# Four post-layernorm layers on one core: state scan with phases in PSUM, stage fronts in another order, recurrence tables made in the first stage

## The reference

```python
for attn, ffn in (
    (causal rope attention, 16 heads of 16;   2-layer local transformer, 8 heads of 64, window 128),
    (attention with relative bias;            projection with mx-quantised values),
    (state scan;                              mixture of 16 routed and 2 shared experts),
    (linear recurrence;                       2-layer local transformer)):
    x = layernorm(x + attn(x))
    x = layernorm(x + ffn(x))
```

```python
# state scan: 32 heads k, 8 channels h, 8 frequencies m
phi = k_val[..., None] * theta
num_re = jnp.cumsum(pwb * jnp.cos(phi), axis=1)
num_im = jnp.cumsum(pwb * jnp.sin(phi), axis=1)
s_re, s_im = num_re * inv, num_im * inv              # inv = 1 / den
out_re = jnp.sum(s_re * qr + s_im * qi, axis=-1)
out_im = jnp.sum(s_im * qr - s_re * qi, axis=-1)
# recurrence, 128 complex states
lam = jnp.exp(-jnp.exp(nu_log) + 1j * jnp.exp(theta_log))
Bu = jnp.einsum('bti,ni->btn', x, B_re + 1j * B_im) * jnp.exp(gamma_log)
states[t] = lam * states[t - 1] + Bu[t]
y = jnp.einsum('btn,on->bto', states, C).real + jnp.einsum('bti,oi->bto', x, D)
```

## Time and profile before

| | us |
|---|---|
| median of 3 runs | 8263.17 (8258.72 to 8267.3) |
| profiled execution | 8261.89 |
| its span | 8260.2 |
| PE busy | 6734.6 (82%) |
| DVE busy | 4886.6 (59%) |
| ACT busy | 2733.4 (33%) |
| POOL busy | 1566.9 (19%) |
| mean granted TensorE clock | 0.911 |

### The profile page before, as it was taken

One profiled execution on the slowest core, in us unless ns is written; L12 is line 12 of the kernel. 1 busy time (PEld: TensorE's weight loads), 2 busy tenths in 40 slices (PEclk: granted clock), 3 DMA queues, 4 the chain that ended last, 5 costly groups with the idle time before them and its releaser, 6 DMA issues. The chain is left out here.

```text
span 8260.2 us, 122768 instructions
## 1 busy us (share of the span) xinstructions
PE 6734.6 (82%) x30724; PEld 3442.2 (42%) x30724; DVE 4886.6 (59%) x12027; ACT 2733.4 (33%) x6003; POOL 1566.9 (19%) x847
## 2 busy tenths in 40 slices
PE   6799958988898866999994486776886689889989
PEld 3233334554465432222223352334443345544554
DVE  3555557634774535777775749994334676337645
ACT  0255524612471101555551113331110146124621
POOL 1111115100510011000000007880000261006100
PEclk9899979999999987999997698998988899999999
...
DMA packets 921871, 833.01 MB, mean 101 GB/s; under 512 B 239752, under 2 KB 786528, under 8 KB 921248
## 3 DMA queue, kind: packets, MB, share of 16 engines
...
...
## 5 line engine op out<-in xcount | busy, mean ns | idle before, releaser
L1216 ACT ACTIVATE Catt_E<-Catt_t 128x512 f32<-128x512 f32 x1024 | 576.8, 596 | 501.6 <-DVE Catt_t L1179 319.7
L1155 DVE CUSTOM_DVE_ANT_0 Catt_S<-Catt_s,Catt_win 128x1024 f32<-128x1024 f32 x512 | 621.3, 1215 | 40.9 <-DMA Catt_win<-skewed 38.8
L1155 DVE CUSTOM_DVE_ANT_0 Aatt_S<-Aatt_s,Aatt_win 128x128 f32<-128x128 f32 (+7 forms) x512 | 377.2, 756 | 325.7 <-PE Aatt_s L1094 320.0
L1137 PE MATMUL Catt_o<-Catt_E,Catt_V 128*32 128x256 f32 (+1 forms) x3840 | 548.6, 404 | 0.0
L1216 ACT ACTIVATE Aatt_E<-Aatt_t 128x512 f32<-128x512 f32 (+3 forms) x768 | 355.4, 489 | 325.5 <-PE Aatt_t L1119 257.4
L1179 DVE TENSOR_TENSOR Catt_t<-Catt_t,Catt_near 128x256 f32<-128x256 f32 (+2 forms) x640 | 281.2, 456 | 261.6 <-PE Catt_t L1116 229.9
L1116 PE MATMUL Catt_t<-Catt_Q,Catt_K 123*128 123x512 bf16 x1024 | 327.9, 388 | 91.9 <-ACT Catt_E L1216 71.8
L1094 PE MATMUL Catt_s<-Catt_K,Catt_Q 96*128 96x512 bf16 x1024 | 324.4, 400 | 46.8 <-DMA Catt_near<-near_s 38.1
L2304 PE MATMUL scan_cum<-scan_X,scan_after 128*128 128x512 f32 x448 | 251.3, 644 | 121.8 <-DVE scan_pr L2373 117.5
L1137 PE MATMUL Aatt_o<-Aatt_E,Aatt_V 128*32 128x256 f32 (+2 forms) x2304 | 324.5, 389 | 0.0
L2306 PE MATMUL scan_cum<-scan_X,scan_upto 128*128 128x512 f32 x512 | 279.0, 637 | 39.5 <-POOL scan_X L2280 23.5
...
## 6 DMA issues: line engine op xcount, KB each, us to landing
...
```

What stands on the lines that cost most here:

```text
L1137: ins = t.matmul(o_ps[f:f + 2 * hd, x:y], V[:, b, kb, h, :], E[:, kb % NB, h, x:y], start=kb == 0, stop=kb == end and y == hi)
L1155: v.tensor_tensor_reduce(out=S[:, j % 2, 0:w], in0=s_ps[j % 2][:, 0:w], in1=win[:, 0 if causal else h, w0:w0 + w], scale=-1.0, scalar=BIG, ...
L1216: a.activation(E[:, kb % NB, h, lo:hi], t_ps[n % 2][:, 0:hi - lo], ACT.Exp, scale=scale).then_inc(exped, 1)
```

## The change

- **State scan.** `ph` moves from SBUF (two buffers) to PSUM (one), `ys` too. Rounding is split: ACT gets `whole`, one pass that adds the large constant (kept in `magic`) to `ph` and writes `nn`, and `fraction` moves to DVE as one instruction that takes the constant off again and subtracts `ph`. POOL keeps `weigh` and `add` alone, and its `weigh` waits for DVE's `weigh` of the same step (`x_done[1]`). The sine half is now summed and read first. One round more of lag lies between `phase` and the rest.
- **Recurrence tables.** A class `RecurrenceTables` makes `ex` and `rot` on DVE and two Sin on ACT within `stage_enter`, and keeps them in SBUF (about 8 KB a partition) to the last layers. Its log load is SP's in `enter`. ACT's and PE's first batch stand outside the loop there. The matching loads and instructions leave the recurrence.
- **Thin attention.** SP's wait for `set_up` goes; Q and K are loaded at once on `head_in`, V (after `V_ones`), `ext` and `near` on a new `late_in`. The three rows of K are filled by DVE (`K_ones`) instead of POOL. With bias the first windows are loaded right behind the first Q and K, and the 24 rows of Q after the second batch's window.
- **Local attention.** V counts on its own semaphore `V_in`, and only the products with V wait for it.
- **Rotary qkv.** SP's order is `w`, the first half of `hT`, then `rt` and the scales on a new `r_in` that only DVE waits for, then the second half.

The core of the diff:

```diff
-def stage_enter(nc, x, act0, acts):
+def stage_enter(nc, x, act0, acts, tables, logs):
...
+            tables.load(sp, logs)
...
-            with s.Fori(0, B) as it:
+            def columns(it):
...
+            columns(0)
+            tables.sines(s)
+            with s.Fori(1, B) as it:
+                columns(it)
...
+        @block.vector
+        def _(v):
+            tables.make(v)
...
-        head_in = [pl.sem(f"head_in{i}") for i in range(B)]
+        head_in, V_in = ([pl.sem(f"{n}{i}") for i in range(B)] for n in ("head_in", "V_in"))
...
-                             ).then_inc(head_in[b], 16)
+                             ).then_inc(V_in[b], 16)
...
-                    t.wait_ge(head_in[b], it * 48 + 48)
+                    t.wait_ge(head_in[b], it * 32 + 32)
...
+                if u == 0:
+                    t.wait_ge(V_in[b], it * 16 + 16)
...
-            sp.wait_ge(set_up, 1)
-            if not causal:
+            def put_of():
...
-                sp.wait_ge(put, 16 * PARTS)
...
-                if b == 1 and not causal:
+                if b == 1 and not causal and not isinstance(it, int):
                     window(it, 0)
                 sp.wait_ge(pv_done, it * nv + (b + 1) * (nv // B))
                 apart(sp, pl.sp_unread)
                 for x, x_s in ((Q, q_s), (K, k_s)):
                     sp.dma_start(x[0:K0, b], x_s.rearrange("f t c -> (f t) c")[bass.ds(it * (2 * K0), 2 * K0), b * T:(b + 1) * T]
                                  .rearrange("(h p) c -> p h c", h=2)).then_inc(head_in[b], 16)
+                if b == 0 and not causal and isinstance(it, int):
+                    window(it, 0)
+                if b == 0 and isinstance(it, int):
+                    sp.wait_ge(V_ones, 1)
                 for h in range(2):
                     sp.dma_start(V[:, b, :, h, 0:hd], v_s[b * T:(b + 1) * T, bass.ds(it * (2 * hd) + h * hd, hd)]
-                                 .rearrange("(t p) d -> p t d", p=P)).then_inc(head_in[b], 16)
+                                 .rearrange("(t p) d -> p t d", p=P)).then_inc(late_in[b], 16)
                 if not causal:
                     sp.dma_start(K[K0 + PARTS:K1, b], ext[bass.ds(it * (2 * PARTS * NT), 2 * PARTS * NT), :]
-                                 .rearrange("(h p) c -> p h c", h=2)).then_inc(head_in[b], 16)
+                                 .rearrange("(h p) c -> p h c", h=2)).then_inc(late_in[b], 16)
                     sp.dma_start(near[:, b], nears[bass.ds(it * (2 * P), 2 * P), :].rearrange("(h p) c -> p h c", h=2)
-                                 ).then_inc(head_in[b], 16)
+                                 ).then_inc(late_in[b], 16)
                 if b == 1 and not causal:
                     window(it, 1)
+                    if isinstance(it, int):
+                        put_of()
...
-            g.memset(V[:], 1.0)
-            g.drain()
-            g.memset(K[K0:K0 + PARTS], 1.0)
+            if causal:
+                CausalWindow().make(g, win[:, 0, :]).then_inc(win_made, 1)
+                g.drain()
+            g.memset(V[:], 1.0).then_inc(V_ones, 1)
             g.drain()
             if causal:
-                CausalWindow().make(g, win[:, 0, :])
-                g.drain()
...
-            t.wait_ge(set_up, 1)
...
-                    t.wait_ge(head_in[b], it * (16 * LOADS) + 16 * LOADS)
+                    t.wait_ge(head_in[b], it * 32 + 32)
...
+                if b == 0 and isinstance(it, int):
+                    t.wait_ge(set_up, 1)
...
+                if i == 0 and isinstance(it, int):
+                    t.wait_ge(K_ones, 1)
+                    if not causal:
+                        t.wait_ge(put, 16 * PARTS)
...
+                    t.wait_ge(late_in[b], it * (16 * LATE) + 16 * LATE)
...
-            v.wait_ge(set_up, 1)
+            v.memset(K[K0:K0 + PARTS], 1.0).then_inc(K_ones, 1)
+            if causal:
+                v.wait_ge(win_made, 1)
...
+            def columns(it, c):
+                sp.wait_ge(v_done, it * NT + (c * 4 + 4))
+                apart(sp, pl.sp_unread)
+                for kt in range(KT):
+                    sp.dma_start(hT[:, c, kt, :], cols_of(act_in, it, c * CH - kt, CH, kt)).then_inc(h_in[c], 16)
+
+            columns(0, 0)
+            sp.dma_start(rt[:], rot.rearrange("(t p) a d -> p t a d", p=P)).then_inc(r_in, 16)
                 for half in range(2):
                     sp.dma_start(sc[:, 2 * a + 1, half * (hd // 2):(half + 1) * (hd // 2)],
-                                 x[(1 - half) * (hd // 2):(2 - half) * (hd // 2)].partition_broadcast(P)).then_inc(w_in, 16)
-            with sp.Fori(0, B) as it:
+                                 x[(1 - half) * (hd // 2):(2 - half) * (hd // 2)].partition_broadcast(P)).then_inc(r_in, 16)
+            columns(0, 1)
+            with sp.Fori(1, B) as it:
                 for c in range(2):
...
+                    columns(it, c)
...
-            t.wait_ge(w_in, 16 * 8)
+            t.wait_ge(w_in, 16)
...
-            v.wait_ge(w_in, 16 * 8)
+            v.wait_ge(r_in, 16 * 7)
...
-        ph, f, nn = pl.sb("ph", [P, 2, W]), pl.sb("f", [P, 2, W]), pl.sb("nn", [P, 2, W])
+        f, nn = pl.sb("f", [P, 2, W]), pl.sb("nn", [P, 2, W])
...
+        ph = pl.ps("ph", (P, W))
+        ys = [pl.ps(f"ys{i}") for i in range(2)]
...
-            def fraction(it, j):
-                n = it * ST + j
-                g.wait_ge(ph_done, n + 1)
-                g.wait_ge(trig_done, n + 1)
-                g.tensor_tensor(f[:, j % 2, :], ph[:, j % 2, :], nn[:, j % 2, :], ALU.subtract).then_inc(f_done, 1)
-
             def weigh(it, m):
+                g.wait_ge(x_done[1], it * ST + (m + 3))
...
             def add(it, m):
-                g.wait_ge(c_used[1], it * ST + (m + 2))
+                g.wait_ge(c_used[0], it * ST + (m + 2))
                 g.tensor_tensor(pr[:, m % 2, :], pr[:, m % 2, :], pi[:, m % 2, :], ALU.add).then_inc(sum_done, 1)
-            pipelined(g, B, ST, ((1, weigh), (0, fraction), (2, add)))
+            pipelined(g, B, ST, ((2, weigh), (3, add)))
...
-                    for i in range(2):
+                    for i in (1, 0):
...
+            def whole(it, j):
+                n = it * ST + j
+                a.wait_ge(ph_done, n + 1)
+                a.wait_ge(f_done, n + 1)
+                a.activation(nn[:, j % 2, :], ph[:], ACT.Identity, bias=magic[:]).then_inc(rounded, 1)
...
-            pipelined(a, B, ST, ((0, trig), (3, store)))
+            pipelined(a, B, ST, ((1, trig), (0, whole), (4, store)))
...
+            def fraction(it, j):
+                n = it * ST + j
+                v.wait_ge(rounded, n + 1)
+                v.wait_ge(trig_done, n + 1)
+                v.scalar_tensor_tensor(out=f[:, j % 2, :], in0=nn[:, j % 2, :], scalar=-MAGIC, in1=ph[:],
+                                       op0=ALU.add, op1=ALU.subtract).then_inc(f_done, 1)
             def phase(it, j):
-                n, g = it * ST + j, j // NT
+                g = j // NT
+                v.drain()
                 v.wait_ge(r_in[j % R], it * (ST // R * 16) + (j // R + 1) * 16)
-                v.wait_ge(f_done, n + 1)
-                v.tensor_tensor(khm(ph[:, j % 2, :]), khm(th[:, g * W:(g + 1) * W]),
+                v.tensor_tensor(khm(ph[:]), khm(th[:, g * W:(g + 1) * W]),
                                 r[:, j % R, 0:P].rearrange("p (k h) -> p k h", k=16).unsqueeze(3).to_broadcast([P, 16, SH, SM]),
-                                ALU.mult)
-                v.drain()
-                v.tensor_scalar(nn[:, j % 2, :], ph[:, j % 2, :], MAGIC, -MAGIC, ALU.add, ALU.add).then_inc(ph_done, 1)
+                                ALU.mult).then_inc(ph_done, 1)
...
-                for i, dst in enumerate((pr, pi)):
+                for i, dst in ((1, pi), (0, pr)):
...
-                v.tensor_reduce(ys[:, j % 2, :], pr[:, j % 2, :].rearrange("p (e m) -> p e m", m=SM), AX_X, ALU.add)
+                v.tensor_reduce(ys[j % 2][:, 0:P], pr[:, j % 2, :].rearrange("p (e m) -> p e m", m=SM), AX_X, ALU.add)
...
-            pipelined(v, B, ST, ((0, phase), (1, weigh), (2, read), (3, reduce)))
+            pipelined(v, B, ST, ((1, fraction), (0, phase), (2, weigh), (3, read), (4, reduce)))
...
+class RecurrenceTables:
...
+    def load(self, sp, logs):
+        sp.dma_start(self.lg[:], logs).then_inc(self.logs_in, 16)
+    def sines(self, a):
+        a.wait_ge(self.trig_in, 1)
+        a.activation(self.rot[:, 1, 1:2], self.wr[:], ACT.Sin)
+        a.activation(self.rot[:, 0, 1:2], self.cr[:], ACT.Sin).then_inc(self.trig_done, 1)
+    def make(self, v):
+        v.wait_ge(self.logs_in, 16)
+        exact_exp(v, self.ex[:], self.lg[:], self.n3[:], self.r3[:], self.p3[:])
...
+        v.tensor_scalar(self.cr[:], self.aw[:], float(np.pi / 2), None, ALU.add).then_inc(self.trig_in, 1)
+        v.memset(self.rot[:, 0, 0:1], 1.0)
+        v.memset(self.rot[:, 1, 0:1], 0.0)
+        v.wait_ge(self.trig_done, 1)
...
```

(14 more changed lines are left out.)

132 lines of the change are left out of this document (65 added, 67 removed).

## The result

The changed kernel takes 8074.15 us in the median of four runs (8060.76 to 8075.08), the one before 8263.94: a ratio of 0.9767, with a 95% interval from 0.975 to 0.9784, or 190 us less. The forecast was 8056 with a range of 8030 to 8105. The profiled execution has a span of 8073.4 us, 186.8 less than before. Two single executions of later runs, one of the kernel before (20870.96 us at a mean granted clock of 0.34) and one of `before_pad` (15169.23 us at 0.48), stand apart from all others and are in none of the ratios.

A forecast was written before the change was run, and what follows sets the result against it. A ring of POOL, DVE and ACT was taken to bound the scan, stage fronts the other touched places. Terms of -120, -22.5, -1.7, -12, -24, -18 and -8.5 sum to -206.7, from 8261.89 to 8055, forecast 8056 (8030 to 8105).

The forecast's parts named there:

- Scan: State scan: the step falls from 9.43 to 7.5 us with DVE as its bound, -120 us.
- DVE's list: State scan: DVE's passes in one step add up to 7.4 us and bound it; 7.5 taken to allow for semaphores.
- Rival 1: State scan: PE becomes the bound, a step of 8.2 us, 75 off in place of 120, total 8101; chance 0.10.
- Rival 2: State scan: POOL's add ends late and DVE meets POOL twice, 9.7 a step, total 8176 to 8192; chance 0.04.
- Recurrence: Recurrence: with `ex` and `rot` ready early, first states come 22.9 us earlier; -22.5 us (-15 to -24).
- `Aatt`: Front of `Aatt`: loads go at once, DVE's fill takes 8.7 us, first mask at about 291; -12 us (-7 to -16).
- `Catt`: Front of `Catt`: first mask 27 us earlier, some 3 come back; -24 us (-10 to -28).
- The late window: `Catt`: the second half's window lands after the ninth mask would want it, giving back some 3 us.
- `enter`: Stage `enter`: two function table loads on ACT in place of four; -1.7 us (+3 to -4).
- Rotary fronts: Four rotary stages: `hT` goes 6 us earlier, the reduce 4.1 to 6 earlier; 4 x -4.5 = -18 us (-8 to -26).
- Local attentions: Four local attentions: first scores no longer wait for V's load; 4 x -2.15 = -8.5 us (-2 to -11).
- the products with V hide it: Local attentions: products with V come later than V's load of 2.15 us, so that load is hidden.

The follow-up runs named there:

- before_pad: The kernel before with 229 empty instructions (drains) added for VectorE in the first stage, `enter`; 8262.3 us against 8253.87, ratio 1.0013.
- pool_free: The changed kernel without POOL's wait for DVE's `X` ahead of its own `X` in the scan; 8154.18 us, ratio 0.9877 to the kernel before.

## Why the prediction came out as it did

**Scan: right**, and the point on which most hung. The sum of DVE's list gave 7.4, taken 7.5, measured 7.46. The one row that no trace had shown, `f`, was taken at 1.3 and took 1.21. The reading that `nn` was held for 2.2 us "in place of 1.1" was wrong in size: its shortest run took 0.69; the sum does not use it. Rival 1 (PE as the bound) did not come: PE was busy 91% and DVE 95%. Rival 2 was a true mechanism, 0.28 us away, and `pool_free` shows it at 8.77 a step.

**Recurrence: right in place, 2 us off in size.** First states 6.3 behind the first products (5.4 taken), first states 23.0 earlier within the stage, and 2.5 of it was given back behind them.

**`Aatt`: the first mask right, the stage not.** It came at 291.12 where 291 was forecast, 11.7 earlier. Two errors cancelled: the fill took 6.88 and not 8.7, nearer to POOL's 6.92 in the earlier trace rows than to DVE's passes; and it began at 284.21, 1.9 behind POOL's first instruction, which the sum left out. The prediction's estimate by the Trainium skill ("VectorE: DVE Perf Modes", section "Zero memsets can be issued as uint32"), 8.5 us, is not borne out: 6.88 was measured, and that decides. The stage kept 7.7: by the starts of the masks in the two traces 1.4 went slowly over the stage and about 2.6 behind the last mask. Eight traces with this front give 771.2 to 774.8 (mean 773.0) and four with the old one 780.3 to 782.5 (mean 781.3), so 8 of the 12 repeat and part of the loss does too.

**`Catt`: the front right, 6 us given back.** 27 earlier at the first mask was forecast and 27.0 came. The late window cost 4.7 instead of 3. The step that failed is the silent one, that a gain at the front stays until the stage's end: within the loop the masks fell back by another 4.4, in steps at the jumps back, where DVE waits 5 us and PE's granted clock falls for a longer or shorter time. Behind the six jumps the clock stood at its lower level for 6.8, 6.8, 10.2, 10.2, 3.4 and 10.2 us in the kernel before and for 10.2 five times and then 3.4 in the changed one; the masks lost 1.8, 2.8, 0, 0 and 3.1 at the first five and got 2.5 back at the sixth. Most of that is chance of the pair of traces and no price of the change: in the eight traces with this front `Catt` takes 1197.1 to 1204.1 (mean 1200.0), in the four with the old one 1219.0 to 1223.0 (mean 1220.5), a gain of 20.5.

**`enter`:** -2.9 instead of -1.7; ACT loads two function tables there instead of four, as was forecast.

**Rotary fronts: right, undersized.** -24 instead of -18. The reduce comes 4.9 to 6.1 us earlier; 4.5 had been taken between bounds of 4.1 and 6. PE's first product comes 5.7 to 6.8 earlier, 24.5 in the four stages, and the stages gained as much as that and more than the reduce's 21.2. The sum took the reduce as what decides; that it is PE's start instead is what the numbers suggest, and no run tests it.

**Local attentions: the term that was wrong.** Each front gave 1.8 to 2.0 of the 2.15 forecast, but the four stages grew by 7.7 us where they were to lose 8.5. The step that failed is "the products with V hide it", as if nothing else in the stage could move. The edit in `enter` moved VectorE's code, and `B1att` lost 12.6. With `before_pad` this is shown, not argued: the same 12 to 16 us come without any edit of the loads. It also explains how the edit of the tables, costed at -1.7 beside `enter`, had a price nine stages and 2200 us later. What `H0att` and `H1att` did (+3.8, -4.3) is scatter: they wait in both kernels.

**Untouched stages.** They were put at zero and sum to -0.1, by luck: `moe` -8.6 comes with the place of its code as well (`before_pad` has it too), but its waits at the jumps are as long at 58, where it stood before, as at 37, where it stands now. In its stage the granted clock stood at the lower level for 113 us before and for 99 in the changed kernel; why is open.

In the traces 187 came of 207. The distance to the forecast of the whole, 18 us in the medians, is as small as it is because misses cancel: the local attentions were 16 worse than forecast, the thin ones 11, the rotary stages 6 better, and every other term stayed within 2.

**Left open.** Single executions of the changed kernel took 8051 and 8061 where its others took 8067 to 8075, and none of them was profiled. Why PE's granted clock falls after nearly equal pauses for 3 us at one jump and for 10 at another was not explained.
